# Mamba layer with routed experts: head and first batch rebuilt (one root for both norms, softplus by halves, C's rows through DRAM, states summed in three banks, other work dealt to other steps)

## The chip, the cores and the metric

One NeuronCore of a Trainium2 chip. The metric is the device time of one execution in microseconds. A core has TensorE (PE, matmuls into eight PSUM banks of 128 x 512 fp32), VectorE (DVE), ScalarE (ACT), GpSimd (POOL) and SyncE (SP, which here only issues transfers). Each engine runs its own instruction list in order; semaphores tie them together.

## The reference

x is 8 batches x 512 times x 128 features. Its layernorm xn goes into two branches, whose results are added to x:

```
a mamba block:
    xh = xn * rsqrt(mean(xn^2) + eps) * norm_w
    xs, z = split(xh @ in_proj.T)                  # 256 channels each
    u = silu(conv4(xs) + conv_b)                   # over time, per channel
    dt, B, C = split(u @ x_proj.T)                 # 8, 16, 16
    delta = softplus(dt @ dt_proj.T + dt_b)
    h[t,:,s] = exp(delta*A[:,s]) * h[t-1,:,s] + delta*u*B[t,s]     # 16 states
    y = sum_s C[t,s] * h[t,:,s] + u * D
    out = (y * silu(z)) @ out_proj.T + xn
eight experts, the two best for each of the 4096 rows (softmax of their two logits):
    out = sum_e gate[e] * (silu(xn @ w_gate[e]) * (xn @ w_up[e])) @ w_down[e]
```

## The kernel before, in words

**Mamba.** Channels lie on the partitions (two halves `hf` of 128), time along the 512 elements. Batches b = 0..7 come one after another, each in 16 steps k, one state each. Step n = 16b + k needs a decay exp(delta*A) (`decay`, `decay_bank` on ScalarE), an input delta*u*B and a scan by VectorE for each half. B's and C's values vary along time alone. They reach 128 partitions in two ways: as columns, when the input is turned (time on partitions), scaled by ScalarE (`scaled`) and turned back by TensorE (`dbu_turn`), or as rows read from DRAM with a broadcast (`rows_in`, `out_rows_in` on SP's queue), when GpSimd multiplies (`scaled` there). Batch 0 and most of batches 6 and 7 take the first way (`BY_PE`), the rest the second.

The sum over states has two forms. In batches 1 to 7 the scan writes in a PSUM bank, VectorE multiplies with C's row (`product`, L1055 to 1064) and TensorE adds the product, turned, in banks 2 and 3 (`accumulate`); `skip` adds u*D there. In batch 0 the scan writes in SBUF (`scan0`), TensorE turns h (`h_turn`), and VectorE multiplies by C's column and adds (`sums`, L1066 to 1078), four instructions a step. At its end `y_evac` (ScalarE) and `y_turn` (TensorE) bring y back to channels, with D's matmul, before `gate`.

**Head.** `stats` and `norms` (VectorE) give mean, 1/sigma and 1/rms for the first 4 tiles of 128 rows (batch 0) and then for the other 28, with two trips to ScalarE's square root each (`root`). VectorE writes xh, GpSimd xn (`normal`) and first the four scaled convolution weights wk. TensorE turns xh (`xh_turn`), ScalarE copies it (`xh_out`), four matmuls (`conv`) for each half make the convolution, then `silu`, `rows` (B, C, dt), `steps_mm` (delta's argument), and softplus as max(v,0) + ln(1 + exp(-|v|)) with a correction for what 1 + y rounds off: `magnitudes`, `vanishing`, `rounded`, `corrected`, `logarithm` on ScalarE, `remainder`, `softplus`, `input_scale` on VectorE for batch 0 and on GpSimd for the rest. `columns` makes the columns of B and C, `input_turn` turns delta*u.

**Routing**, in batch 0's steps: logits by TensorE; `choices` (VectorE, step 4) finds the two best of 8; GpSimd makes `sel`; TensorE `totals` and `ranking` (steps 5, 6), each copied by ScalarE (`routing`). GpSimd then works out each row's slot, the one-hot `hi_val` for half of the groups and each tile's expert (`texp`), L795 to 826. VectorE makes the other one-hots (`one_hots`, steps by `HOT_STEP`), TensorE multiplies them (`inverse`, `MAP_STEP`), `sources` gives the gather lists. Only after its chain does GpSimd work on batch 1: `remainder`, `softplus`, `input_scale`, `scaled(S)`, then it loads the first expert inputs. 72 expert tiles of 128 rows run beside the steps, one a step, from (b=1, k=2) to (5, 9) (`SLOTS`); SP loads their weights when `texp` is known. From (5, 14) on GpSimd gathers the results.

**Order.** Every engine's list is written out by step: `step0(k)` for batch 0 and `step(b, k)` for the others stand once per engine, and a table such as `HOT_STEP`, `SLOTS`, `COLS_AT` says in which step a piece is dealt with. `ST_LN`, `ST_RSTD` and so on count VectorE's small norm instructions for those who wait for one. SP's list: x in four parts (the second waits for ScalarE's five constant loads, `FIRST`), ten constants (`REST`), xn's rows to DRAM, rows of batch 1, weights. What sets a step's pace in the banked form:

```
wait(act, "p_rdy", freed(b, m))                       # L495: a decay waits for the product that read its bank
act.wait_ge(s["h_rdy"], 2 * IN_SBUF[i - ND] + hf + 1) # L452: one of three SBUF decays is free
wait(dve, "acc_mm", 2 * (S * (b - 1) + k - 1))        # L1060: a product waits for the sum two steps back
```

## Time and profile before

| | before |
|---|---|
| median of 3 runs | 686.74 us (684.6 to 687.96) |
| profiled execution | 688.27 us, span 686.4 us |
| busy share: PE, DVE, ACT, POOL | 80%, 89%, 63%, 77% |
| mean granted TensorE clock | 0.913 |
| chain that ended last, by engine | PE 41%, DVE 20%, ACT 15%, POOL 11%, issue 11%, DMA 3% |
| HBM read, written | 108.21 MB, 9.37 MB |

The time of an execution is its span, from the first to the last instruction, and a little around it. A row of a timeline gives the start in us from the span's start, the length from the first to the last of the instructions that it merges, engine, line, operation, tiles, shapes and count; in brackets the idle time before it and what ended it. A row of windows gives the stretch, its length, the busy time (and instructions) of PE, PE's weight loads, DVE, ACT and POOL, the granted clock, the DMA engines' busy share and GB/s. `bank` stands for any of the eight PSUM banks. A line of a helper serves several batches. The granted clock is 1.00 for TensorE's upper level, 2.4 GHz, and 0.50 for its lower, 1.2 GHz. A single matmul of fp32 shows as two instructions.

### The profile page before, as it was taken

Reading aid. Unit: us, or ns where it says so; the run is one execution under the profiler, and the core shown is the slowest. Engines: PE = TensorE matmul, PEld = TensorE weight load, DVE = VectorE, ACT = ScalarE, POOL = GpSimd, SP = SyncE. Lnnn points to the kernel's source line nnn. Section 1 sums busy time; section 2 is a strip of 40 time slices with the busy share of each in tenths; the row PEclk is TensorE's granted clock in tenths of the full one; section 3 lists DMA queues with packets and bytes.
Section 4 is the critical chain, followed back from the end, with each engine's and each line's share of the span. In section 5 each row is a group of like instructions: output and inputs, shape, how many; then the busy total and the mean of one; then the engine's idle time right before and its main releaser. Section 6 shows DMA issues by size and latency. Waiting matters only on the chain.

```text
span 686.4 us, 11312 instructions
## 1 busy us (share of the span) xinstructions
PE 547.6 (80%) x3456; PEld 425.1 (62%) x3456; DVE 613.3 (89%) x901; ACT 433.2 (63%) x849; POOL 528.8 (77%) x535
## 2 busy tenths in 40 slices
PE   2778767648879998899979998899887675687787
PEld 1256555435767877678767777687665454574554
DVE  6674888997998999999999999999999988888776
ACT  2498787614765576565765586657664689578680
POOL 5596059987988879896989879897869879758670
PEclk9958887767989999999999999999999897889987
DMA  6120040050776687687877687777843343223621
GB/s 203 54 62 16 1 187 1 0 192 16 255 249 236 230 288 252 211 251 275 290 251 267 236 302 265 227 278 232 295 145 147 147 157 141 81 78 108 161 77 31
DMA packets 58283, 118.32 MB, mean 172 GB/s; under 512 B 8200, under 2 KB 39440, under 8 KB 51440
## 3 DMA queue, kind: packets, MB, share of 16 engines
q1 hardware_dynamic: 53008, 107.83, 45.1%
q0 software_dynamic: 4496, 9.45, 5.4%
q8 instruction: 28, 0.46, 0.3%
q10 hardware_dynamic: 720, 0.33, 0.2%
q14 instruction: 31, 0.25, 0.1%
HBM read 108.21 MB, written 9.37 MB: 171 GB/s over the span
## 4 chain that ended last, share of the span: by engine, by line
PE 41%; DVE 20%; ACT 15%; POOL 11%; issue 11%; DMA 3%; DVEq 0%; ACTq 0%; POOLq 0%
DVE bank L1052 7%; PE bank L1330 7%; PE bank L1424 7%; PE bank L1306 5%; POOL dbu L845 5%; PE bank L1438 4%; PE bank L1432 4%; POOL xhT L874 3%; DVE h_sb L1063 3%; ACT dbu L487 3%; PE bank L1262 2%; ACT da L456 2%; PE bank L1353 2%; DVE h_sb L1034 2%; DMA xhT<-y_slots,slot 2%
## 5 line engine op out<-in xcount | busy, mean ns | idle before, releaser
L845 POOL TENSOR_TENSOR dbu<-du,xn_all 128x512 f32<-128x512 f32 x178 | 223.5, 1278 | 46.4 <-DVE bank L1052 45.9
L1052 DVE TENSOR_TENSOR_SCAN bank<-bank,dbu 128x512 f32<-128x512 f32 x176 | 214.2, 1221 | 4.1 <-ACT bank L471 4.1
L471 ACT ACTIVATE bank<-delta,a_sb 128x512 f32<-128x512 f32 x176 | 121.6, 692 | 99.1 <-DVE h_sb L1063 77.6
L1063 DVE TENSOR_TENSOR h_sb<-bank,xh_all 128x512 f32<-128x512 f32 x224 | 148.8, 676 | 1.1
L1306 PE MATMUL bank<-id_sb,h_sb 128*128 128x128 f32 x864 | 118.6, 283 | 16.8 <-DVE h_sb L1063 13.7
L1306 PEld LDWEIGHTS bank<-id_sb,h_sb 128*128 128x128 f32 x864 | 102.2, 147 | 25.9 <-DVE h_sb L1063 19.2
L1424 PEld LDWEIGHTS bank<-wd_sb,hid 117*128 117x128 f32 (+1 forms) x432 | 56.1, 194 | 64.1 <-issue 33.0
L1424 PE MATMUL bank<-wd_sb,hid 117*128 117x128 f32 (+1 forms) x432 | 66.0, 290 | 32.3 <-ACT xT L628 18.3
L1262 PE MATMUL bank<-id_sb,dbu 128*128 128x128 f32 x304 | 52.6, 315 | 38.0 <-ACT dbu L487 21.0
L832 POOL DMA_INDIRECT xs<-xn_rows,src x72 | 70.8, 983 | 14.2 <-issue 7.3
L1262 PEld LDWEIGHTS bank<-id_sb,dbu 128*128 128x128 f32 x304 | 40.4, 162 | 60.6 <-ACT dbu L487 31.9
L1330 PE MATMUL bank<-xhT,wk_sb 128*128 128x512 f32 x128 | 69.3, 673 | 1.7 <-ACT xhT L430 0.8
L1052 DVE TENSOR_TENSOR_SCAN bank<-da,bank 128x512 f32<-128x512 f32 x46 | 54.6, 1217 | 16.7 <-PE bank L1262 11.3
L487 ACT ACTIVATE dbu<-du_t,bc_sb 128x256 f32<-128x256 f32 x152 | 64.3, 496 | 1.3 <-PE bank L1262 1.2
L1432 PE MATMUL bank<-xT,wgu_sb 128*118 128x128 f32 x432 | 60.6, 277 | 4.2 <-DVE ga L1105 4.2
L456 ACT ACTIVATE da<-delta,a_sb 128x512 f32<-128x512 f32 x80 | 53.8, 713 | 13.5 <-DVE h_sb L1034 7.0
L1438 PE MATMUL bank<-xT,wgu_sb 128*118 128x128 f32 x432 | 60.5, 276 | 0.0
L1432 PEld LDWEIGHTS bank<-xT,wgu_sb 128*118 128x118 f32 x432 | 52.9, 184 | 6.6 <-issue 6.5
L874 POOL DMA_INDIRECT xhT<-y_slots,slot x48 | 46.7, 974 | 12.4 <-issue 11.7
L1438 PEld LDWEIGHTS bank<-xT,wgu_sb 128*118 128x118 f32 x432 | 53.9, 185 | 0.8 <-issue 0.8
L634 ACT ACTIVATE th<-bank 118x384 f32<-118x384 f32 x72 | 34.8, 484 | 29.3 <-PE bank L1432 26.9
L1034 DVE TENSOR_TENSOR_SCAN h_sb<-da,bank 128x512 f32<-128x512 f32 x30 | 34.9, 1202 | 18.4 <-issue 7.6
(191 smaller groups left out, 938.0 us busy)
## 6 DMA issues: line engine op xcount, KB each, us to landing
xh_all<-b_rows SPq DMA_DIRECT2D x28, 1024.0 KB
xn_all<-b_rows SPq DMA_DIRECT2D x25, 1024.0 KB
wgu_sb<-in_w_gu SPq DMA_DIRECT2D x72, 352.0 KB
wd_sb<-in_w_dn SPq DMA_DIRECT2D x72, 192.0 KB
y_slots<-ys SPq DMA_DIRECT2D x72, 64.0 KB
xn_rows<-xn_all SPq DMA_DIRECT2D x8, 256.0 KB, 2.3
out<-x_sb SPq DMA_DIRECT2D x7, 256.0 KB
x_sb<-in_x SPq DMA_DIRECT2D x2, 640.0 KB, 5.8
```

Of the source, the lines that this page charges most:

```text
L471: nc.scalar.activation(bank_of(b, m)[:, :], delta[b % 2][:, hf, :], ACT.Exp, scale=a_sb[:, hf, k:k + 1]).then_inc(s["da_rdy"], 1)
L487: last = nc.scalar.activation(dbuT[k % 2][:, t, :], duT[:, t, :], ACT.Copy, scale=bc_sb[q][:, t, k:k + 1])
L832: nc.gpsimd.indirect_dma_start(xs[i][:, :], None, xn_rows, bass.IndirectOffsetOnAxis(ap=src[:, j:j + 1], axis=0)).then_inc(s[f"xs_in{i}"], 16)
L845: nc.gpsimd.tensor_tensor(dbu[k % 2][:, hf, :], du[b % 2][:, hf, :], b_ring[c % 2][:, k % CH, :], ALU.mult).then_inc(s["dbu_p"], 1)
L1052: nc.vector.tensor_tensor_scan(at, da_of(n)[:, hf, :] if n in IN_SBUF else at, inp, 0.0, ALU.mult, ALU.add).then_inc(s["h_rdy"], 1)
L1063: nc.vector.tensor_tensor(h_sb[k % 2][:, hf, :], bank_of(b, 2 * k + hf)[:, :], c_ring[c % 2][:, k % CH, :], ALU.mult).then_inc(s["p_rdy"], 1)
L1262: last = nc.tensor.transpose(at[:, t * P:(t + 1) * P], dbuT[k % 2][:, t, hf * P:(hf + 1) * P], id_sb[:, :])
L1306: last = MM(HT[i][:, t % 2, hf * P:(hf + 1) * P], h_sb[k % 2][:, hf, t * P:(t + 1) * P], id_sb[:, :], is_transpose=True, start=(k == 0 and ...
L1330: last = MM(at[:, :], wk_sb[:, tap, hf * P:(hf + 1) * P], xhT[:, c, tap:tap + T], start=(tap == 0), stop=(tap == K - 1))
L1424: last = MM(XD[:, P:P + H], hid[j % 2][0:FN[c], c * P:(c + 1) * P], wd_sb[j % NW][0:FN[c], c, :], start=(c == 0), stop=(c == NF - 1))
L1432: last = MM(GB[0:FW, c * P:(c + 1) * P], wgu_sb[j % NW][:, c * FS:c * FS + FW], xT[j % 2][:, :], start=True, stop=True)
L1438: last = MM(UB[0:FW, c * P:(c + 1) * P], wgu_sb[j % NW][:, F + c * FS:F + c * FS + FW], xT[j % 2][:, :], start=True, stop=True)
```

## The change

It rewrites the head and batch 0; the 16 steps of the other batches keep their form.

- Norms: both variances (var + eps, and var*(1+eps') + eps*eps', under the root of which stands the product of both norms) go through one root, as a [128, 2, n] tensor. xh's scale is one of the two results. The 28 later tiles' rows are written in three parts (up to tile 24 in the head, 24 to 27 in step 0, 28 to 31 in step 1). 1/rms is worked out in step 1.
- The constants are loaded in another order; TensorE's and GpSimd's first wait is for three (`FIRST`), not five. The first convolution takes its taps from the last to the first, as GpSimd finishes them.
- Softplus of batch 0: by halves. ScalarE does Abs, Exp and Ln; VectorE max(v,0) from the bank, 1+y, the correction. Convolutions of batch 1 stand before the input is turned; its SiLU becomes tanh and a VectorE `unit`.
- Batch 0's state sum takes the form of the other batches, with three banks (0, 1, 5) as batches 6 and 7 have. C's rows for steps 0 to 7 come from DRAM in four pieces of two rows (512 KB spread over 128 partitions each) in buffers that are free then (`own`); those for steps 8 to 15 in `c_ring`. D is added by `skip` in steps 10 and 11.
- `choices` moves from step 4 to 7, totals and ranking from 5, 6 to 8, 9, one-hots from 9 to 14 to 12 to 15, the last two inverses and `sources` in step (1,0). Batch 1's softplus on GpSimd goes ahead of the routing chain, the first expert loads after step (1,0).
- Expert tiles start at (1,4) and end at (5,11). The columns of batch 6 are made two steps later.

The diff, cut to what this text speaks of:

```diff
-    TURNED, SKIPPED = 11, (1, 2)
+    TURNED, SKIPPED, SKIPPED0 = 11, (1, 2), (10, 11)
     LN_EPS = 1e-5
     RMS_EPS = float(np.finfo(np.float32).eps)
-    ST_LN, ST_RMS, ST_RSTD, ST_NORM = 7, 15, 12, 22
+    ST_ROOT, ST_NORM = 6, 13
+    XH_HEAD = 24
...
-        SLOTS = [(1, k) for k in range(2, S)] + [(b, k) for b in (2, 3, 4) for k in range(S)] + [(5, k) for k in range(10)]
+        SLOTS = [(1, k) for k in range(4, S)] + [(b, k) for b in (2, 3, 4) for k in range(S)] + [(5, k) for k in range(12)]
...
-        HOT_STEP = {9: (0, 1), 10: (2,), 11: (3,), 12: (4, 5), 13: (6,), 14: (7,)}
-        MAP_STEP = {10: (0, 1), 11: (2,), 12: (3,), 13: (4, 5), 14: (6,), 15: (7,)}
+        HOT_STEP = {12: (0, 1), 13: (2, 3), 14: (4, 5), 15: (6, 7)}
+        MAP_STEP = {13: (0, 1), 14: (2, 3), 15: (4, 5)}
+        def b_turn(k):
+            return {0: 4, 2: 5, 3: 6, 5: 7}.get(k)
...
-        COLS_AT = {5: 13, 6: 14}
+        COLS_AT = {5: 15, 6: 14}
...
-            return {9: 1, 12: 0} if b == 0 else {8: 1, 10: 0} if b == 6 else {4: 1, 6: 0}
+            return {13: 1, 15: 0} if b == 0 else {8: 1, 10: 0} if b == 6 else {4: 1, 6: 0}
...
-            return DAB2[m % 2] if b < 6 else DAB3[m % 3]
+            return DAB2[m % 2] if 0 < b < 6 else DAB3[m % 3]
...
+        own = [delta[1][:, 0:2, :], du[1][:, 0:2, :], g_sb[:, 0:2, :], u_sb[2][:, 0:2, :]]
...
-        FIRST, REST = 16 * 5, 16 * 10
+        FIRST, REST = 16 * 3, 16 * 10
...
+            def own_rows(i):
+                if i == 0:
+                    sp.wait_ge(s["b_st"], 16)
+                    sp.wait_ge(s["w_scaled"], 5)
+                spread_rows(own[i].rearrange("p s t -> p (s t)"), S + 2 * i, 2).then_inc(s[f"c_own{i}"], 16)
...
+            rows_kept(0)
+            rows_out(0)
+            for i in range(4):
+                own_rows(i)
+            for b in range(1, 4):
+                rows_kept(b)
+            sp.wait_ge(s["xh_pe"], 4)
+            out_rows_in(0, 2)
+            for b in range(4, NB):
+                rows_kept(b)
             rows_out(1)
+            sp.wait_ge(s["xh_pe"], NB)
+            out_rows_in(0, 3)
...
+            for dst, src_of in ((win_sb[:, :], w_in), (nw_sb[:, :], norm_w), (id_sb[:, :], ident)):
                 act.dma_start(dst, src_of).then_inc(s["in_first"], 16)
+            for dst, src_of in ((cb_sb[:, :], conv_b), (dtb_sb[:, :], dt_b)):
...
+                if 0 < k < S - 1:
+                    scaled(k + 1)
                 if k + 2 < S:
                     decay(k + 2)
                 elif k + 1 == S:
                     decay_bank(S, 0)
-                if 0 < k < S - 1:
-                    scaled(k + 1)
+                if b_turn(k) is not None:
+                    xh_out(b_turn(k))
+                if k in (0, 2):
+                    half_tanh(1, k // 2)
+                if k == 4:
+                    rows(1)
+                if k in (5, 6):
+                    magnitudes(1, k - 5)
+                    vanishing(1, k - 5)
+                if k == 6:
+                    rounded(1)
+                    corrected(1)
+                if k == 7:
+                    logarithm(1)
+                if k in (8, 11):
+                    half_tanh(2, k // 11)
...
+            def first_logarithm(hf):
+                act.wait_ge(s["sp_one"], hf + 1)
+                nc.scalar.activation(sp_e[:, hf, :], sp_d[:, hf, :], ACT.Ln).then_inc(s["sp_ln"], 1)
...
             silu(0, 0)
...
+            root(ST_NORM + ST_ROOT, slice(TT, NT))
             silu(0, 1)
...
             xh_out(1)
...
             act.wait_ge(s["in_rest"], REST)
             nc.scalar.activation(a_sb[:, :, :], a_sb[:, :, :], ACT.Exp).then_inc(s["a_ready"], 1)
...
+            rows(0)
+            xh_out(2)
+            for hf in range(NH):
+                magnitudes(0, hf)
+                vanishing(0, hf)
+            nc.scalar.activation(cbh_sb[:, :], cb_sb[:, :], ACT.Copy, scale=0.5)
             act.wait_ge(s["a_ready"], 1)
             nc.scalar.activation(a_sb[:, :, :], a_sb[:, :, :], ACT.Copy, scale=-1.0).then_inc(s["a_ready"], 1)
...
+            act.wait_ge(s["w_scaled"], 6)
+            first_logarithm(0)
+            first_logarithm(1)
             columns(0)
...
             act.wait_ge(s["a_ready"], 2)
             decay(0)
+            xh_out(3)
             input_turned(0)
             scaled(1)
             decay(1)
...
             for k in range(S):
...
+            remainder(pool, nc.gpsimd, 1)
             pool.wait_ge(s["oh_out"], 1)
             nc.gpsimd.tensor_tensor(sel[:, :, :], oh1, oh2, ALU.add).then_inc(s["sel_rdy"], 1)
             rt(nc.gpsimd.tensor_tensor(kk[:, :], m2[:, :], m1[:, :], ALU.subtract))
             nc.gpsimd.tensor_tensor(kk[:, :], kk[:, :], irms[:, :], ALU.mult).then_inc(s["top_rdy"], 1)
+            softplus(pool, nc.gpsimd, 1, 1)
+            input_scale(pool, nc.gpsimd, 1, 1)
             pool.wait_ge(s["rk_out"], 1)
...
+            def first_loads():
+                pool.wait_ge(s["xn_out"], 16 * NB)
+                pool.wait_ge(s["src_rdy"], 1)
+                for j in range(NXS - 1):
+                    load(j)
...
+                    if b == 1 and k == 0:
+                        first_loads()
...
+                var, a = [v[:, sl] for v in tmp]
+                under, root, inv, b = [v[:, :, sl] for v in both]
                 begun = cnt[0]
                 dve.wait_ge(s["stats_bn"], n1)
...
                 st(nc.vector.tensor_tensor(a, me, mo, ALU.subtract))
...
+                st(nc.vector.tensor_tensor(var, stat[:, sl, 2], stat[:, sl, 5], ALU.add))
                 st(nc.vector.scalar_tensor_tensor(a, a, 0.25, a, ALU.mult, ALU.mult))
...
+                st(nc.vector.scalar_tensor_tensor(var, var, 1.0 / H, a, ALU.mult, ALU.add))
+                st(nc.vector.tensor_scalar(both[0][:, 0, sl], var, LN_EPS, None, ALU.add))
+                st(nc.vector.tensor_scalar(both[0][:, 1, sl], var, 1.0 + RMS_EPS, LN_EPS * RMS_EPS, ALU.mult, ALU.add))
+                assert cnt[0] == begun + ST_ROOT
+                st(nc.vector.tensor_tensor(mean[:, sl], me, mo, ALU.add))
+                st(nc.vector.tensor_scalar(mean[:, sl], mean[:, sl], 0.5, None, ALU.mult))
+                dve.wait_ge(s["rms_rt"], roots)
+                st(nc.vector.reciprocal(inv, root))
+                st(nc.vector.tensor_tensor(b, inv, inv, ALU.mult))
+                st(nc.vector.tensor_tensor(b, b, under, ALU.mult))
+                st(nc.vector.tensor_scalar(b, b, -0.5, 1.5, ALU.mult, ALU.add))
+                st(nc.vector.tensor_tensor(inv, inv, b, ALU.mult))
...
+                if b == 0 and c < 2:
+                    if k % 2 == 0 and hf == 0:
+                        dve.wait_ge(s[f"c_own{k // 2}"], 16)
+                    row = own[k // 2][:, k % 2, :]
+                else:
+                    if k % CH == 0 and hf == 0:
+                        dve.wait_ge(s[f"c_in{c % 2}"], 16 * ((b - 1) * 2 + c // 2 + 2) if b else 16)
+                    row = c_ring[c % 2][:, k % CH, :]
                 if hf == 0:
...
+                    wait(dve, "acc_mm", 2 * (S * b + k - 1))
                 dve.wait_ge(s["h_rdy"], 2 * (b * S + k) + hf + 1)
...
+                nc.vector.tensor_tensor(h_sb[k % 2][:, hf, :], bank_of(b, 2 * k + hf)[:, :], row, ALU.mult).then_inc(s["p_rdy"], 1)
...
             def step0(k):
-                scan0(k)
-                if k > 0:
-                    sums(k - 1)
+                scan(0, k, 0)
+                scan(0, k, 1)
+                product(0, k, 0)
+                product(0, k, 1)
+                if k == 0:
+                    rows_normed(XH_HEAD, NT - TT)
+                if k == 1:
+                    rows_normed(NT - TT, NT)
+                    st(nc.vector.reciprocal(irms[:, :], sxh))
+                    st(nc.vector.tensor_tensor(irms[:, :], irms[:, :], rstd, ALU.mult))
+                if k in (0, 2):
+                    unit(1, k // 2)
+                if k == 7:
+                    choices()
+                if k in (8, 11):
+                    unit(2, k // 11)
+                if k == 10:
+                    weights()
                 if k in z_step(0):
                     z_gate(0, k)
-                if k == 4:
-                    choices()
-                if k == 10:
-                    weights()
                 for r in HOT_STEP.get(k, ()):
                     one_hots(ORDER[r])
-                if k in (11, 14):
-                    unit(2, k // 14)
-                if k == S - 1:
-                    sources()
...
+                if b == 1 and k == 0:
+                    sources()
...
+            relu(0)
+            one_more(0)
+            lost(0)
+            relu(1)
+            one_more(1)
+            regained(0)
+            lost(1)
+            first_step(0)
+            input_scale(dve, nc.vector, 0, 0, (0,))
+            regained(1)
+            first_step(1)
+            input_scale(dve, nc.vector, 0, 0, (1,))
             dve.wait_ge(s["row_mm"], 1)
-            for hf in range(NH):
-                dve.wait_ge(s["du_rdy"], hf + 1)
-                nc.vector.tensor_tensor(dbu[0][:, hf, :], du[0][:, hf, :], DBU[0][:, :], ALU.mult).then_inc(s["dbu_0"], 1)
+            first_input(0)
+            first_input(1)
...
             def step0(k):
                 if k > 0:
...
+                    dbu_turn(0, k, (1,))
+                    accumulate(k - 1)
+                if k + 1 < S:
+                    dbu_turn(0, k + 1, (0,))
                 for r in MAP_STEP.get(k, ()):
                     inverse(r)
                 if k == 1:
...
+                    conv(1, 1, range(K))
+                if k == 3:
                     rows(1)
...
+                if k == 7:
+                    conv(2, 0, range(K))
+                if k == 8:
+                    totals()
+                if k == 9:
+                    ranking()
+                if k in (9, 10):
+                    conv(2, 1, (2 * k - 18, 2 * k - 17))
                 if k + 1 in z_step(0):
                     z_mm(0, k)
...
+                if k in SKIPPED0:
+                    skip(0, (SKIPPED0.index(k),))
+                if b_turn(k) is not None:
+                    xh_turn(b_turn(k))
+                    logits(b_turn(k) - 1)
+                if k == 6:
+                    logits(NB - 1)
+                if k in (4, 5):
+                    steps_mm(1, k - 4)
...
             def step(b, k):
                 g = b * S + k
                 prev, here, nxt, nn = tile(g - 1), tile(g), tile(g + 1), tile(g + 2)
                 if k == 0:
-                    if b > 1:
-                        accumulate(g - 1)
+                    accumulate(g - 1)
+                    if b == 1:
+                        inverse(6)
+                        inverse(7)
...
-            pe.wait_ge(s["w_scaled"], 5)
-            pe.wait_ge(s["x_pad"], 2)
             pe.wait_ge(s["xhT_c"], 1)
             for hf in range(NH):
-                conv(0, hf, range(K))
+                conv(0, hf, range(K - 1, -1, -1))
+            xh_turn(1)
             rows(0)
-            xh_turn(1)
+            xh_turn(2)
             for hf in range(NH):
                 steps_mm(0, hf)
+            MM(bank[0][:, :], id_sb[0:2 * S, 0:1].to_broadcast([2 * S, P]), bct_full[0:2 * S, :],
+               start=True, stop=True).then_inc(s["row_mm"], 1)
             logits(0)
-            MM(DBU[0][:, :], id_sb[0:2 * S, 0:1].to_broadcast([2 * S, P]), bct_full[0:2 * S, :],
-               start=True, stop=True).then_inc(s["row_mm"], 1)
+            logits(1)
             columns(0)
-            logits(1)
-            xh_turn(2)
+            conv(1, 0, range(K))
+            xh_turn(3)
             input_turn(0, 0)
             logits(2)
-            xh_turn(3)
             for k in range(S):
                 step0(k)
             for b in range(1, NB):
```

## Rows read from the trace of the kernel before

**Rows 1.** Windows, all engines: head, batch 0; the third: batch 7's sixteen steps.

```profile
0.00:48.06 48.06, 26.90 (x63) 13.33 (x64) 32.18 (x118) 23.53 (x33) 31.74 (x49) 0.82 0.38 110
48.06:156.51 108.45, 77.81 (x443) 56.91 (x441) 89.04 (x135) 69.46 (x126) 72.59 (x96) 0.81 0.18 65
...
611.43:679.30 67.87, 52.34 (x283) 36.77 (x282) 56.66 (x68) 46.80 (x105) 42.67 (x55) 0.90 0.33 93
```

**Rows 2.** Timeline of VectorE, head and first steps: start, us, operation [idle before].

```profile
6.40 0.17 DVE L950 TENSOR_SCALAR tmp<-tmp 128x4 f32<-128x4 f32 x1
...
12.05 1.27 DVE L963 TENSOR_SCALAR xh_all<-x_sb,mean,sxh 128x128 f32<-128x128 f32 x4
...
30.18 7.88 DVE L963 TENSOR_SCALAR xh_all<-x_sb,mean,sxh 128x128 f32<-128x128 f32 x28
...
44.35 1.29 DVE L406 TENSOR_TENSOR delta<-sp_d,sp_m 128x512 f32<-128x512 f32 x2 [1.07 <-ACT sp_d L692]
...
57.57 2.33 DVE L1034 TENSOR_TENSOR_SCAN h_sb<-da,bank 128x512 f32<-128x512 f32 x2 [7.16 <-PE bank L1262]
```

**Rows 3.** Timeline of TensorE in the head.

```profile
14.63 6.66 PE L1330 MATMUL bank<-xhT,wk_sb 128*128 128x512 f32 x8 [0.78 <-ACT xhT L430]
22.07 3.70 PE L1330 MATMUL bank<-xhT,wk_sb 128*128 128x512 f32 x8 [0.78 <-ACT u_sb L645]
...
31.98 3.77 PE L1353 MATMUL bank<-bct_full,dtw_sb 8*128 8x512 f32 x4
```

**Rows 4.** Groups of VectorE over batch 0: name, count, busy us, mean ns, idle before.

```profile
L1077 DVE SCALAR_TENSOR_TENSOR g_sb<-bank,bc_sb,g_sb 128x256 f32<-128x256 f32 x56 | 22.8, 468 | 0.0
L1002 DVE TENSOR_TENSOR lo_oh<-lanes_sb,lo 128x1024 f16<-128x1024 f32 x8 | 11.4, 1432 | 0.0
```

**Rows 5.** Timeline of GpSimd, from the head to the end of its routing chain.

```profile
7.82 0.48 POOL L748 TENSOR_SCALAR wk_sb<-sp_e,nw_sb 128x256 f32<-128x256 f32 x1 [4.99 <-DMA dtb_sb<-in_dt_b]
...
91.38 0.20 POOL L795 TENSOR_SCALAR tiles<-wgu_sb 128x8 f32<-128x8 f32 x1 [5.77 <-ACT wgu_sb L441]
...
101.47 12.15 POOL L820 TENSOR_SCALAR hi_val<-lanes_sb,hi 128x72 f16<-128x72 f32 x16 [0.23 <-POOL lo L813]
...
136.96 2.49 POOL L387 TENSOR_TENSOR sp_m<-sp_m,sp_y 128x512 f32<-128x512 f32 x2
139.41 3.49 POOL L393 TENSOR_TENSOR sp_m<-sp_m,sp_e 128x512 f32<-128x512 f32 x2
```

**Rows 6.** Transfers issued in the first 60 us: KB each, median us to landing.

```profile
xn_rows<-xn_all SPq DMA_DIRECT2D x8, 256.0 KB, 2.3
...
g_sb<-in_conv_w POOLq DMA_DIRECT2D x1, 512.0 KB, 5.9
```

**Rows 7.** Timeline of ScalarE: the head's table load, two groups of a step.

```profile
41.97 1.28 ACT L692 ACT_TABLE_LOAD   x1
...
66.14 1.69 ACT L487 ACTIVATE dbu<-du_t,bc_sb 128x256 f32<-128x256 f32 x4
...
68.21 1.32 ACT L456 ACTIVATE da<-delta,a_sb 128x512 f32<-128x512 f32 x2
```

**Rows 8.** Timeline of VectorE in batch 7: scans of two successive steps.

```profile
614.86 2.33 DVE L1052 TENSOR_TENSOR_SCAN bank<-da,bank 128x512 f32<-128x512 f32 x2
...
618.28 2.33 DVE L1052 TENSOR_TENSOR_SCAN bank<-da,bank 128x512 f32<-128x512 f32 x2
```

**Rows 9.** Timeline of VectorE in batch 0: an instruction of `choices`.

```profile
79.28 0.42 DVE L974 TENSOR_REDUCE m<-wgu_sb 128x32 f32<-128x256 f32 x1
```

**Rows 10.** Windows of TensorE: busy, granted clock (share of full), DMA share, GB/s.

```profile
86.00:88.00 2.00, 2.00 (x11) 0.50 0.13 33
```

**Rows 11.** Groups of GpSimd up to the end of batch 0: busy, mean ns, waits.

```profile
L820 POOL TENSOR_SCALAR hi_val<-lanes_sb,hi 128x72 f16<-128x72 f32 x32 | 23.3, 750 | 2.1 <-PE bank L1245 1.8 <-POOL lo L813 0.2
```

**Rows 12.** Timeline of VectorE, first steps of batch 1.

```profile
156.51 1.22 DVE L1052 TENSOR_TENSOR_SCAN bank<-bank,dbu 128x512 f32<-128x512 f32 x1
...
163.69 1.28 DVE L1086 TENSOR_TENSOR g_sb<-zs_sb,bank 128x512 f32<-128x512 f32 x2 [3.29 <-PE bank L1390]
...
168.62 1.22 DVE L1052 TENSOR_TENSOR_SCAN bank<-bank,dbu 128x512 f32<-128x512 f32 x1
```

324 lines of the change are left out of this document (114 added, 210 removed).

## The prediction

> **What bounds the kernel now.** I read first how long each batch takes. The first scan starts at 48.06 us, batch 0 ends at 156.51, and in these 108.45 us VectorE is busy for 89.04 only [rows 1]. What follows, 530 us for seven batches, is nearly untouched by the diff. So the two prologue stretches are the question: 48.06 and 108.45 us, of 686.4.
>
> In the head the reader is to see a single chain that goes round VectorE, ScalarE, TensorE and GpSimd: the first normalised rows are written at 12.05, the other 28 only at 30.18, and delta only at 44.35; then scan 1 waits 7.16 us for its transposed input [rows 2]. TensorE runs its first convolution half from 14.63 in 6.66 us, the second from 22.07 in 3.70, the step matmuls of both halves from 31.98 in 3.77 [rows 3]. The first 6.66 and the 3.77 are slow for their size: the engine was at the lower level there.
>
> In batch 0 each step costs VectorE two scans and four sums; 56 of the 64 sum instructions keep it busy for 22.8 us, so all 64 for 26.1 [rows 4]. Last I read GpSimd's routing chain: it starts at 91.38, when the ranks are out of the bank, and gives way to the next batch's softplus at 136.96, 45.6 us later [rows 5].
>
> **The head.** (1) One root for both norms: 6 instructions before the root in place of 7, 7 after it (2 of them hidden beside it) in place of 16, and no second trip to ScalarE. The last instruction before the first root starts at 6.40; one of 0.2 us less before it, root and hand-overs of 0.4, then five of 0.2: the first rows can start at about 8.0, against 12.05 [rows 2]. Three transfers in place of five gate the scaled weights, whose first instruction starts at 7.82 on GpSimd [rows 5]; but the taps, 512 KB, take 5.9 us to land [rows 6] from their issue at the start, so I take only 0.5 us there. Some VectorE instructions next to GpSimd's get longer, so rows at 8.3 and the convolution at 10.9, against 14.63: 3.7 us won. The taps in falling order hide what is left of the scaling. (2) The convolution halves stay 6.66 and 3.70 [rows 3]: they end at about 22. (3) The second root waits behind the first SiLU, so the other rows come at about 21 in place of 30.18 [rows 2]; the turned inputs of the next batches, which stood in front of the step matmuls, no longer wait for them. B and C's rows are in SBUF at about 26. (4) Softplus by halves: step matmul about 1 us at the upper level (1.9 in the trace, 3.77 for two [rows 3]), then ScalarE Abs and Exp for each half, 4 x 0.65 (two 128x512 instructions take 1.32), one table load of 1.28 and two Ln halves of 0.6 [rows 7]: the logarithms are done at about 32.5. Relu, 1+y and the correction run on VectorE meanwhile. After the first Ln half come seven VectorE instructions at 0.64 (1.29 for two [rows 2]), 4.5 us: scan 0 at about **37**, 11 us earlier. If TensorE works at the lower level again, as it did for the 3.77, two step matmuls and the columns behind them cost 2 to 3 us more.
>
> C's rows need a store and a load by DRAM. The store waits for the 26 above. The nearest rows are a store of 256 KB, 2.3 us to landing, and the load of the taps to all partitions, 512 KB as each of these four, 5.9 us [rows 6]. That puts the first pair in SBUF at 35, and the first product is due at 39.5. Cost 0; if the four loads queue behind each other, 4 x 5.9 us is still before step 6. At most 3 us, which I keep for the range.
>
> **Batch 0.** (5) VectorE: 89.04 busy, less 26.1 of sums, plus 32 products. A step of two scans and two products in this very form is in batch 7: 614.86 to 618.28 is 3.42 us [rows 8], so the products add 16 x 1.2 = 19. Moved in: 8 normalised rows at 0.28 (7.88 for 28 [rows 2]), two u multiplications and the reciprocal, 4 us. The one-hots ran 1.43 us at a mean where 1.22 is their quick length [rows 4], since GpSimd's softplus ran beside them; that softplus is earlier now: 4 us less with their companions. Sum 82: VectorE alone would need 82 us where 108.45 stood.
>
> (6) It won't be alone. ScalarE has for every step four scaled copies (1.69) and two decays (1.32), 2.9 us when they follow each other closely [rows 7]; to these come in steps 0 to 7 fifteen 128x512 instructions of about 0.65 (inputs turned, half-tanhs, the magnitudes of batch 1), two of 1.15 and a Ln with its table: 14.4 us. So 38 us in eight steps, against VectorE's 8 x 3.42 + 4 = 31. I work each step through its queue: product k-1 frees the bank, TensorE sums it and turns the next input, ScalarE delivers one step ahead. Scan 1 starts 8 us after scan 0 (in place of 9.5), step 7 ends at about 73. `choices` then costs 12 instructions at 0.42 with 0.03 between them [rows 9], 5.4: about 78.
>
> (7) From there the routing sets the end. GpSimd makes `sel`, TensorE totals, ScalarE copies, TensorE ranks, ScalarE copies. Before, the second instruction of `choices` began at 79.28, so it ended near 84.3, and 91.38 is 7 us later [rows 5, 9]; now ScalarE has a half-tanh, scaled copies and decays in between, and TensorE has stood idle during `choices`, after which its granted clock was 0.50, the lower level [rows 10]. I take 10.5: ranks out at **88.5**. Of the 45.6 us of GpSimd's chain 2.1 were waits, 1.8 of them for slots [rows 11]; the rest stays: about 43.5. Softplus of batch 1 is past by then, so `scaled(S)` follows at once and its first half takes 1.3. Batch 1's first scan: 88.5 + 43.5 + 1.5 = **133.5**, against 156.51. VectorE has finished batch 0 at about 127 and waits 6 us. So 23 us won, 11 in the head, 12 in batch 0.
>
> The GpSimd row to weigh here: its `hi_val` instructions take 12.15/16 = 0.76 us each in their first sixteen, and the correction, with one-hots beside it, takes 1.75 each where the sum before it takes 1.25 [rows 5]. The Trainium skill (GPSIMD Engine Reference, Specifications) says that GpSimd shares its SBUF interfaces with VectorE and contends with instructions that have two SBUF inputs; the trace agrees, and the change now packs all one-hots into steps 12 to 15.
>
> **After batch 0.** (8) The end of the state sum no longer waits for four `sums`, a y turned and a D matmul: the gate's wait of 3.29 before 163.69 goes [rows 12]. But `sources` now follows the gate, and GpSimd makes four gathers after it and then the input of step 2: about 12 us to step 2, as before (156.51 to 168.62 [rows 12]). 0. (9) Two expert tiles move from steps (1,2), (1,3) to (5,10), (5,11). A step with a tile is longer than one without by the same amount at either place, as VectorE paces both: net 0. But the gather of slots keeps its step, two steps after the last tile in place of four, and the columns of batch 6 come two steps later, behind which TensorE turns batch 6's input. 1 to 2 us, taken as 1.5. SP's added transfers (a store, six row loads) stand before waits that are met anyway. The row loads are bounded by nothing and 3 us.
>
> **Sum**, against the profiled execution's 688.27 (span 686.4): -23 + 1.5 = -21.5, so 666.8. That execution lies 1.5 above the median 686.74; against the median it gives **665**.
>
> **Rivals.** *VectorE sets the end of batch 0* (0.18): the routing hand-overs take the old 7 us and the queue is level, step 7 ends at 70: VectorE's 82 us plus 5 of stalls, a start at 126 to 128. 659. For it: VectorE was the busiest engine of batch 0 [rows 1].
> *Port sharing stretches GpSimd's chain* (0.13): 16 us of two-input one-hots beside `hi_val` and the 8 expert comparisons, each longer by 1.75/1.25: 16 x 0.4 = 6 us more on the very chain that sets the end. 671. The rule of the Trainium skill (GPSIMD Engine Reference, Key points) would give this; against it, most of the 45.6 us already include such overlap.
> *The loop of three banks paces the steps* (partial 0.12; fully 0.04). Scan k needs a bank freed by a product, filled by TensorE, from ScalarE's copy. Batch 7, the same form, takes 67.87 us with 56.66 busy [rows 1]: 11.2 us idle in 16 steps. The same on top of my queues gives +8, 673. If every step lost 1.6 us beyond my working, 16 x 1.6 = 25 us, the whole gain is gone; at 2 us, 697 at a start of 166: **slower**. It decides from 1.6 us a step. Batch 7 shows 0.7.
> *The gain doesn't arrive* (0.03): expert weights or gathers are late in batch 1 and VectorE stands there; about 685.
>
> **Numbers.** Main case 0.50, 660 to 671. Together with the faster rival and the partial one, and the bounds above (3 for rows, 3 for the clock, 3.5 for hand-overs), 655 to 676 holds 8 in 10. Over 0.5%, 3.4 us, is what a measurement here can tell: faster 0.93, same 0.04, slower 0.03.
>
> **What would show it.** First rows near 8.3, scan 0 near 37, the first product without a wait for C's rows; step 7 ends near 73; ranks out near 88.5; VectorE's long wait at batch 1's first scan ended by GpSimd's `dbu`; batches 2 to 4 as long as before. Wrong if VectorE's wait there is absent (rival one), if the `hi_val` instructions average above 0.9 us (rival two), or if VectorE idles in every step for TensorE or ScalarE (rival three).

## The result and the profile after

| | before | after |
|---|---|---|
| median of 20 executions each | 686.95 us (682.66 to 692.81) | 682.92 us (672.99 to 690.37) |
| profiled execution, span | 688.27, 686.4 us | 673.05, 671.2 us |
| mean granted TensorE clock | 0.913 | 0.919 |

The forecast was 665 (655 to 676). The changed kernel's twenty times fall into two groups with nothing between them: ten from 672.99 to 680.1 and ten from 685.74 to 690.37. The medians of all stand at 682.92/686.95 = 0.994. The ratio with an interval, 0.9857 [0.9833, 0.988], leaves the upper ten out, as every ratio here does with executions over 1.5% above the fastest. The profiled execution is of the lower group, and is one of its three shortest (the median of the ten is 676.7); it shows the steps of the forecast undisturbed. The upper group is the main finding.

Windows of after, all engines (head, batch 0, batch 7), to be read against [rows 1]:

```profile
0.00:37.95 37.95, 24.67 (x77) 12.30 (x78) 29.08 (x97) 19.23 (x29) 24.05 (x39) 0.96 0.60 173
37.95:141.03 103.08, 77.50 (x457) 59.05 (x455) 86.34 (x113) 65.22 (x126) 78.79 (x105) 0.82 0.18 65
594.00:665.60 71.60, 53.05 (x287) 37.99 (x288) 59.23 (x72) 49.19 (x109) 42.49 (x55) 0.93 0.32 89
```

The head won 10.1 us (48.06 to 37.95), its clock in these rows rose from 0.82 to 0.96 (they show 1.00 up to 17.3 us, yet the first five instructions of the convolution stand 0.85 us apart and the later ones 0.43, so TensorE still began at its lower level); batch 0 won only 5.4 (108.45 to 103.08). VectorE is 84% busy there, against 82% before.

Timeline of after, the rows that answer to [rows 2, 3, 5, 12]:

```profile
10.26 1.17 DVE L993 TENSOR_SCALAR xh_all<-x_sb,mean,both 128x128 f32<-128x128 f32 x4
12.72 5.95 PE L1387 MATMUL bank<-xhT,wk_sb 128*128 128x512 f32 x8 [0.69 <-ACT xhT L461]
19.45 3.70 PE L1387 MATMUL bank<-xhT,wk_sb 128*128 128x512 f32 x8 [0.78 <-ACT u_sb L674]
22.58 5.58 DVE L993 TENSOR_SCALAR xh_all<-x_sb,mean,both 128x128 f32<-128x128 f32 x20
37.95 2.37 DVE L1072 TENSOR_TENSOR_SCAN bank<-da,dbu 128x512 f32<-128x512 f32 x2
40.23 1.26 DVE L1089 TENSOR_TENSOR h_sb<-bank,delta 128x512 f32<-128x512 f32 x2
...
78.60 0.41 DVE L1002 COPY wgu_sb<-bank 128x256 f32<-128x256 f32 x1
...
102.79 27.18 POOL L856 TENSOR_SCALAR hi_val<-lanes_sb,hi 128x72 f16<-128x72 f32 x32 [0.23 <-POOL lo L849]
...
141.03 1.23 DVE L1072 TENSOR_TENSOR_SCAN bank<-bank,dbu 128x512 f32<-128x512 f32 x1 [7.56 <-POOL dbu L881]
...
153.39 1.23 DVE L1072 TENSOR_TENSOR_SCAN bank<-bank,dbu 128x512 f32<-128x512 f32 x1 [3.30 <-POOL dbu L881]
```

Scan 0 stands at 37.95, the first product follows without a wait for C's rows, `choices` begins at 78.60, and VectorE's long wait ends with GpSimd's `dbu`: the forecast's picture, 7.5 us late.

### The profile page after: what moved, and what is told of

Same layout as the page of the kernel before. It is cut to its first block, busy times and chain, and to the rows that moved or that the text cites. A ratio compares the mean times of both kernels' runs of the same rounds, so it can differ in the third digit from the quotient of the medians.

```text
span 671.2 us, 11273 instructions
## 1 busy us (share of the span) xinstructions
PE 540.2 (80%) x3468; PEld 425.2 (63%) x3468; DVE 607.5 (91%) x859; ACT 424.4 (63%) x841; POOL 528.3 (79%) x535
## 4 chain that ended last, share of the span: by engine, by line
PE 42%; ACT 19%; DVE 15%; POOL 13%; issue 11%; DMA 1%; DVEq 0%; ACTq 0%; POOLq 0%
DVE bank L1072 7%; PE bank L1481 7%; PE bank L1387 7%; PE bank L1355 6%; ACT dbu L514 5%; PE bank L1495 4%; POOL dbu L881 4%; PE bank L1489 4%; POOL hi_val L856 4%; ACT da L486 4%; DVE h_sb L1089 3%; PE bank L1318 2%; PE bank L1410 2%; PE bank L1456 2%; PE bank L1367 1%
## 5 line engine op out<-in xcount | busy, mean ns | idle before, releaser
L1355 PE MATMUL bank<-id_sb,h_sb 128*128 128x128 f32 x992 | 144.2, 293 | 24.2 <-DVE h_sb L1089 13.1
L1089 DVE TENSOR_TENSOR h_sb<-bank,xh_all 128x512 f32<-128x512 f32 x240 | 160.3, 682 | 1.2
L1355 PEld LDWEIGHTS bank<-id_sb,h_sb 128*128 128x128 f32 x992 | 123.0, 152 | 36.8 <-DVE h_sb L1089 20.9
L1072 DVE TENSOR_TENSOR_SCAN bank<-da,bank 128x512 f32<-128x512 f32 x76 | 90.2, 1217 | 23.0 <-PE bank L1318 21.5
L1318 PE MATMUL bank<-id_sb,dbu 128*128 128x128 f32 x304 | 55.0, 313 | 38.3 <-DVE h_sb L1089 20.5
L1387 PE MATMUL bank<-xhT,wk_sb 128*128 128x512 f32 x128 | 64.3, 634 | 1.5 <-ACT u_sb L674 0.8
L486 ACT ACTIVATE da<-delta,a_sb 128x512 f32<-128x512 f32 x80 | 54.1, 712 | 8.6 <-DVE bank L1072 6.0
L910 POOL DMA_INDIRECT xhT<-y_slots,slot x48 | 46.6, 971 | 14.9 <-issue 11.5
L667 ACT ACTIVATE ys<-bank 128x128 f32<-128x128 f32 x72 | 19.8, 274 | 39.9 <-PE bank L1481 28.9
```

The lines of the kernel that those rows point to most:

```text
L486: nc.scalar.activation(da_of(n)[:, hf, :], delta[b % 2][:, hf, :], ACT.Exp, scale=a_sb[:, hf, k:k + 1]).then_inc(s["da_rdy"], 1)
L1072: nc.vector.tensor_tensor_scan(at, da_of(n)[:, hf, :] if n in IN_SBUF else at, inp, 0.0, ALU.mult, ALU.add).then_inc(s["h_rdy"], 1)
L1089: nc.vector.tensor_tensor(h_sb[k % 2][:, hf, :], bank_of(b, 2 * k + hf)[:, :], row, ALU.mult).then_inc(s["p_rdy"], 1)
L1318: last = nc.tensor.transpose(at[:, t * P:(t + 1) * P], dbuT[k % 2][:, t, hf * P:(hf + 1) * P], id_sb[:, :])
L1355: last = MM(HT[i][:, t % 2, hf * P:(hf + 1) * P], h_sb[k % 2][:, hf, t * P:(t + 1) * P], id_sb[:, :], is_transpose=True, start=(k == 0 and ...
L1387: last = MM(at[:, :], wk_sb[:, tap, hf * P:(hf + 1) * P], xhT[:, c, tap:tap + T], start=(tap == taps[0] if c == 0 else tap == 0), stop=(ta ...
```

## The experiments

Each line of medians is compared with before on the same chip. On some chips before takes 687 to 688, on others 679: theories are told apart within a chip. "Before takes" names the median of the kernel before on that chip.

### The changed kernel again, and GpSimd's input put first

The first has no edit. The second takes the inputs of steps (1,0) and (1,1) out from behind the expert comparisons:

```diff
+            scaled(S)
+            scaled(S + 1)
             for e in range(E):
                 rt(nc.gpsimd.tensor_scalar(tkey[:, :, e], ...
...
-            scaled(S)
```

> The changed kernel once more, unchanged, to see how its times spread and whether batch 1 always starts where the first trace shows it (141.0 us). Theory A (GpSimd's routing chain sets the start of batch 1, and little else differs): 673 to 680 us in each run, batch 1's first scan at 141 with VectorE's wait of 7.6 us before it ended by GpSimd's dbu. Theory B (something apart from the chain takes about 14 us in many runs, as the times from 673 to 690 suggest): two clusters, near 675 and near 688, and if a trace of the upper cluster is seen, a stall of 10 us or more that the first trace does not have.

> Batch 1's first two inputs are multiplied by GpSimd ahead of the eight expert comparisons (9.7 us), and the first four gathers are dealt to steps (1,1) to (1,3). Theory A (the chain sets the start): the first scan of batch 1 comes at 133.5 to 135 in place of 141, the wait before it shrinks from 7.6 to about 1 us, and the time falls by 3 to 6 us against the unchanged one (some is given back at the third step, which waits for the comparisons and its own input). Rival (VectorE or TensorE have no slack there, or the later batches set the time): the same time within 1 us. Theory B says nothing on the first scan, but keeps two clusters 14 us apart.

Measured, where before takes 679.0: 680.48 (671.67 to 683.61), 0.9992 [0.9947, 1.0037]; and 672.27 (three executions at 667.5 to 667.7, three at 676.8 to 680.8), 0.9891 [0.9836, 0.9946]. The six times of the unchanged kernel (671.67, 677.63 and four from 680.08 on) decide nothing between A and B; its trace is of the shortest, with the first scan of batch 1 at 140.68. The second kernel has two groups again, 9 to 13 us apart, and this time the profile caught the upper one, so it can't show what theory A expected of the first scan. Its time is not in waits: up to batch 1's gate VectorE idles less than in the trace of after (22.6 us against 25.8), but is 11.7 us longer busy (130.8 against 119.1), 8.4 of it in one instruction. The timelines of VectorE and GpSimd at this place, first the kernel with the input first (upper group), then after (lower group), then GpSimd in before:

```profile
49.78 9.52 DVE L996 TENSOR_SCALAR xh_all<-x_sb,mean,both 128x128 f32<-128x128 f32 x4
49.81 8.64 POOL L803 TENSOR_TENSOR x_sb<-x_sb,xn_all 128x512 f32<-128x512 f32 x7
59.22 0.34 DVE L1146 RECIPROCAL irms<-both 128x32 f32<-128x32 f32 x1
59.38 1.26 POOL L803 TENSOR_TENSOR x_sb<-x_sb,xn_all 128x512 f32<-128x512 f32 x1 [0.93 <-DVE xh_all L996]
```

```profile
49.10 2.66 DVE L993 TENSOR_SCALAR xh_all<-x_sb,mean,both 128x128 f32<-128x128 f32 x4
50.41 9.90 POOL L803 TENSOR_TENSOR x_sb<-x_sb,xn_all 128x512 f32<-128x512 f32 x8
52.06 0.91 DVE L1144 TENSOR_TENSOR irms<-irms,both 128x32 f32<-128x32 f32 x1
```

```profile
52.68 9.90 POOL L770 TENSOR_TENSOR x_sb<-x_sb,xn_all 128x512 f32<-128x512 f32 x8
```

And the rows of the line alone, with the shortest, median and longest of its 32 instructions, in the same order:

```profile
L996 DVE TENSOR_SCALAR xh_all<-x_sb,mean,both x32: 332/390/8750, 10.4 to 59.0; 128x128 f32<-128x128 f32 x32
```

```profile
L993 DVE TENSOR_SCALAR xh_all<-x_sb,mean,both x32: 332/390/1335, 10.3 to 50.4; 128x128 f32<-128x128 f32 x32
```

One instruction that takes 0.39 us took 8.75, the first of the last four rows. It began beside the first of GpSimd's eight sums x + xn, seven of which follow each other without a gap, and it ended when the seventh did; the eighth needs these four rows, so GpSimd paused, and both went on. In after it was the last of the four that met the first sum, and it lost that sum only, 1.33 us. The profile calls VectorE busy throughout. In before these rows were all written by 38.1 (30.18 + 7.88 [rows 2]) and GpSimd's sums began at 52.68: the two could not meet. The change moved the last rows into step 1.

### Taking the rows out of the meeting, and forcing them into it

Theory H (a hold) says that this one instruction makes the upper group.

```diff
+            pool.wait_ge(s["xh_w"], NT)
             for b in range(NB):
                 pool.wait_ge(s["xh_w"], b * TT + TT)
```

> Edit: GpSimd starts its eight sums of x and xn only when VectorE has written all normalised rows. It adds a wait of about 1 us to an engine that is idle from 60 to 73 us. Theory H (a hold): in the run of 676.84 VectorE's last rows began after GpSimd's first 128x512 sum and one of them took 8.75 us instead of 0.39, which is the whole upper group of times; the changed kernel's own upper group has the same cause. H expects every run in one group, at the changed kernel's lower times: 671 to 676, about 8 under the unchanged one's median of that chip and with a far smaller spread than 12 us; VectorE's rows at 49 us of 0.33 to 0.39 each. Rival N (noise of the chip or its clock, and the hold is rare): the same two groups, 672 and 680 to 684, and a ratio near 1.00 to before.

```diff
                 if k == 1:
+                    dve.wait_ge(s["acc_w"], 1)
                     rows_normed(NT - TT, NT)
```

> Edit: VectorE's last four normalised rows of step 1 wait until GpSimd has ended the first of its eight sums, so they always arrive in the middle of the chain. H: one of the four rows is held until the chain pauses before its eighth sum, 6 x 1.24 = 7.4 us, and the wait for the first sum adds 1 to 2.5; every run is in the upper group, 8 to 10 above the lower one: 681 to 685 in all runs, none under 679. N, or a hold of one instruction of GpSimd only: a row of 1.3 us, 674 to 677 in the lower runs.

The same with, in GpSimd's loop:

```diff
             for b in range(NB):
+                if b > 1:
+                    pool.wait_ge(s["acc_w"], b)
```

> Edit: as the one before, and each of GpSimd's sums after the second waits for the end of the one before it, so that the queue is not back to back. H in its strong form (the row waits for the end of GpSimd's running instruction, and only instructions that follow without a gap keep it out): the row gets in at the first gap and takes 1.3 to 2.6 us; times as the kernel with the wait for all rows plus 2 to 4. H in its weak form (GpSimd's sums keep VectorE's row out whatever stands between them): a row of some 7 to 8 us, and times of the upper group.

> Edit: the kernel that puts GpSimd's input of steps (1,0) and (1,1) ahead of the expert comparisons, with the wait of GpSimd's sums for all rows. H expects all runs at that kernel's lower times, 667 to 669, ratio to before 0.983; N expects its two groups again, 667.6 and 677 to 681.

All on one chip, before 687.6:

| kernel | median, all executions | ratio |
|---|---|---|
| sums wait for all rows | 677.0 (675.5 to 678.8) | 0.9859 [0.9822, 0.9895] |
| rows forced into the sums | 686.58 (684.9 to 690.8) | 0.9987 [0.9958, 1.0017] |
| forced, sums with gaps | 683.93 (680.9 to 686.0) | 0.9950 [0.9922, 0.9978] |
| input first, sums wait | 672.99 (671.3 to 675.4) | 0.9793 [0.9756, 0.983] |

H holds in all four: one group each, of the kind that it says. The medians of the first, second and fourth lie 1 to 4 us above the ranges given for them. With the rows kept out of the sums, every execution is in the lower group; forced together, ten of ten are in the upper. The unchanged kernel's upper group was never profiled itself, but it stands where the forced one does, which makes a hold in it very likely, though none was seen there. Timelines of the two forced kernels:

```profile
51.00 8.64 POOL L803 TENSOR_TENSOR x_sb<-x_sb,xn_all 128x512 f32<-128x512 f32 x7
52.31 8.18 DVE L993 TENSOR_SCALAR xh_all<-x_sb,mean,both 128x128 f32<-128x128 f32 x4 [2.27 <-POOL x_sb L803]
```

```profile
50.62 10.56 POOL L805 TENSOR_TENSOR x_sb<-x_sb,xn_all 128x512 f32<-128x512 f32 x8
51.91 5.32 DVE L995 TENSOR_SCALAR xh_all<-x_sb,mean,both 128x128 f32<-128x128 f32 x4 [2.32 <-POOL x_sb L805]
```

Without gaps one row is held 7.41 us, six sums. With a gap of 0.08 us between the sums (1.34 us from one to the next in place of 1.23) each of the four rows gets in at the next gap, 1.29 to 1.43 us each. The strong form of H stands, though my price for it was low: the time came out 6.9 us above the kernel whose sums wait, where I expected 2 to 4, because all four rows are held in turn (5.32 for 1.1) and the wait for the first sum adds 2.3.

The added wait of GpSimd takes only the rows out of the meeting. The 128x32 product for 1/rms, which comes behind them and takes 0.19 us alone, still runs into the first sum. Timeline of the kernel whose sums wait:

```profile
50.99 9.88 POOL L804 TENSOR_TENSOR x_sb<-x_sb,xn_all 128x512 f32<-128x512 f32 x8 [0.42 <-DVE xh_all L994]
51.20 1.11 DVE L1145 TENSOR_TENSOR irms<-irms,both 128x32 f32<-128x32 f32 x1
```

It began 0.21 us into the first sum here and in the seven other traces of kernels with this wait in which the two meet, and lost that one sum (1.10 to 1.12 us) each time. So the wait gives the meeting a fixed place where it was cheap; it doesn't remove it.

### Only the rows moved; the one-hots doubled; the experts on VectorE

```diff
-                    rows_normed(XH_HEAD, NT - TT)
+                    rows_normed(XH_HEAD, NT)
                 if k == 1:
-                    rows_normed(NT - TT, NT)
                     st(nc.vector.reciprocal(irms[:, :], sxh))
```

> Edit: the changed kernel with nothing but its last four normalised rows moved from step 1 of batch 0 to step 0, beside the twenty others' last four, 8 us before GpSimd's sums begin; no wait added. H: one group of times, the same as with the added wait: ratio to before 0.985 to 0.987, spread under 5 us, no VectorE row above 0.8 us. If the upper group had another cause that the added wait only happened to cover, half of the runs stand 8 to 12 us higher again.

This expectation fell: 674.53 (670.3 to 681.4), eight executions at 670 to 677 and four at 680 to 681.4, 0.9914 [0.9881, 0.9947], where before takes 678.5. The profiled one is of the upper four:

```profile
50.31 9.86 POOL L803 TENSOR_TENSOR x_sb<-x_sb,xn_all 128x512 f32<-128x512 f32 x8
50.53 0.35 DVE L1142 RECIPROCAL irms<-both 128x32 f32<-128x32 f32 x1
50.91 9.31 DVE L1143 TENSOR_TENSOR irms<-irms,both 128x32 f32<-128x32 f32 x1
```

The rows were gone, but the product behind them, with two inputs in SBUF, met the sums in their place: 9.31 us for 0.19. So it is not one instruction: a one-input row and a two-input product were both held. The 1/rms product is also what the wait of the sums leaves in their way. The reciprocal in front of it, one input of 128x32 in SBUF, began 0.22 us into the same first sum and kept its 0.35 us. VectorE's scans and products h x C, each with one input in a PSUM bank, keep their 1.22 and 0.68 us beside the same sums.

The doubled one-hots, on top of the kernel whose sums wait (the added one goes into scratch):

```diff
+                st(nc.vector.tensor_tensor(sp_e[...], lane128..., spread(lo[...])..., ALU.is_equal))
                 nc.vector.tensor_tensor(lo_oh[:, sl, :], ..., ALU.is_equal).then_inc(s["lo_rdy"], 1)
```

> Edit: on top of the kernel whose sums wait for all rows, each of VectorE's eight lo_oh comparisons of 128x1024 is issued twice (the first into scratch). It adds 8 x 1.25 = 10 us to VectorE. Theory P (GpSimd's routing chain was 3.5 us longer than predicted because its hi_val instructions, 0.58 us apart where nothing meets them, wait for VectorE's one-hots): the hi_val group grows from 27.2 to 32 to 36 us and batch 1's first gate moves from 146.4 to 151 to 154. Rival V (VectorE itself sets the end, GpSimd's chain does not care): hi_val stays at 27, VectorE's end of batch 0 moves by 10 against a slack of 7.6, and the gate by 2 to 3, to 149.

678.9, ratio 0.9995 [0.9969, 1.0021]. Groups of GpSimd in its trace:

```profile
L857 POOL TENSOR_SCALAR hi_val<-lanes_sb,hi 128x72 f16<-128x72 f32 x32 | 32.3, 1032 | 0.2 <-POOL lo L850 0.2
L860 POOL TENSOR_SCALAR wgu_sb<-lanes_sb,ends 1x72 f32<-1x72 f32 x8 | 8.7, 1093 | 0.7
```

against 27.2 and 6.7 in after, and 23.3 before [rows 11]. Theory P stands: 10 us more of VectorE's one-hots made GpSimd's chain from the ranks to `dbu` 54.1 us long (97.09 to 151.15) where after has 46.95 and the kernel whose sums wait 46.45 (94.69 to 141.14). The gate stands at 156.38, later than either theory said, since this chain also began 4.4 us later than in after.

Putting the input first, on top of the wait, won 4.0 us on one chip (677.0 to 672.99), but not where theory A had it: the first scan of batch 1 stands at 142.70 in its trace, against 142.54, and the input of step (1,2) comes 3.2 us earlier (151.65 for 154.89). The next two edits look at that first scan. The expert choice (eight comparisons, a tree, a minimum) on VectorE, on top of both edits, and then GpSimd's `dbu` behind VectorE's last one-hot:

```diff
+                st(nc.vector.tensor_tensor(tkey, lanes..., ends[1][0:1, E:2 * E]..., ALU.is_ge))
+                st(nc.vector.tensor_reduce(tsum[:, :], tkey, AX.X, ALU.add))
+                nc.vector.tensor_scalar(texp[:, 0:NJ], tsum[:, :], float(E - 1), None, ALU.min)...
```

```diff
+            pool.wait_ge(s["hi_rdy"], 4)
             scaled(S)
             scaled(S + 1)
```

> Edit: on top of the kernel with both edits (sums wait for all rows; GpSimd's input of steps (1,0) and (1,1) ahead of the expert comparisons), the eight comparisons, the three-level sum and the minimum that give each tile its expert leave GpSimd (10.1 us there) for VectorE: one comparison of 1x576, one reduction, one minimum, 1.6 us, in step 12 of batch 0. GpSimd goes from hi_val straight to dbu and then to the gathers. Theory H (a two-input VectorE instruction that arrives while GpSimd's 128x512 products follow each other waits for all of them): one of VectorE's last one-hots again takes about 6 us, as the 6.40 one of the kernel with both edits; the first scan of batch 1 then stands near 142 and only the later waits for dbu go: 1 to 3 us won against that kernel's 673.0 on the chip of that run (ratio to before 0.976). Rival: the 6.40 us one-hot was a chance meeting; first scan near 137, ratio 0.970.

> Edit: the kernel with the expert choice on VectorE, and GpSimd waits with dbu until VectorE's last one-hot of batch 0 is written. H: VectorE's one-hots take 1.22 each again, they end near 135, dbu's first half is there 1.3 us later and the first scan of batch 1 stands at 136 to 137: 5 us before the kernel without this wait, ratio to before 0.969 to 0.971. Rival (no hold between these two): the wait only delays dbu, and the kernel is 1 us slower than the one without it.

666.28 (662.8 to 670.0), 0.9795 [0.9754, 0.9835], and 664.63 (662.6 to 665.9), 0.9775 [0.9743, 0.9807], with before at 678.5. Both gains are smaller than expected (0.976 and 0.969 to 0.971). The hold shows again at this second place. Timeline of VectorE, without and with the wait:

```profile
134.18 5.79 DVE L1030 TENSOR_TENSOR lo_oh<-lanes_sb,lo 128x1024 f16<-128x1024 f32 x2
141.34 1.23 DVE L1077 TENSOR_TENSOR_SCAN bank<-bank,dbu 128x512 f32<-128x512 f32 x1
```

```profile
131.24 2.35 DVE L1031 TENSOR_TENSOR lo_oh<-lanes_sb,lo 128x1024 f16<-128x1024 f32 x2
136.59 1.23 DVE L1078 TENSOR_TENSOR_SCAN bank<-bank,dbu 128x512 f32<-128x512 f32 x1 [1.54 <-POOL dbu L877]
```

One of the two one-hots took 4.65 us, and 6.40 in the kernel with both edits; behind the wait both are quick and the scan stands at 136.6, as forecast. The gap between the medians, 1.65 us, is less than the 4.75 between these scans, of which 1.4 lay in the head, and the two intervals overlap: the traces show the hold gone, the times don't show what that is worth.

### Which queue paces steps 0 to 7

```diff
-                if k in (0, 2):
-                    half_tanh(1, k // 2)
+                if k in (1, 2):
+                    half_tanh(1, k // 2)
```

and `unit` on VectorE likewise; then also the z gate of (0,15) behind the one-hots.

> Edit: on top of the kernel with the expert choice on VectorE and the wait for its last one-hot, ScalarE's half-tanh and VectorE's u of (batch 1, half 0) move from step 0 to step 1 of batch 0. In the trace of that kernel VectorE stands 3.70 us before this u (45.32) while the bank of scan 1 is turned at 41.74. Theory Q (the pace of the first steps is set by what is queued in front of scan 1, not by TensorE or VectorE): scan 1 starts at 42.0 to 43.5 in place of 45.99, the end of choices moves by 1 to 3 us and so does the end: 662 to 664 on a chip where that kernel takes 664.6. Rival S (ScalarE's queue paces steps 0 to 7, which holds the same instructions in either order): scan 1 earlier, choices within 0.7 us of 79 to 84 as before, no change of the time beyond 1 us.

> Edit: on top of the one before, the z gate of step (0,15) goes behind VectorE's last one-hots. There it waited 0.68 for ScalarE's tanh, and it needs neither the shared path nor GpSimd's dbu, so it fills VectorE's wait of 1.54 for dbu. First scan of batch 1 1.3 to 1.5 us earlier after the end of choices; ratio against the one before 0.998.

666.48, 0.9812 [0.9781, 0.9842], and 667.77, 0.9838 [0.9815, 0.9862]. VectorE in the first of them:

```profile
41.96 1.23 DVE L1078 TENSOR_TENSOR_SCAN bank<-da,bank 128x512 f32<-128x512 f32 x1 [0.24 <-PE bank L1326]
...
49.14 5.40 PE L1395 MATMUL bank<-xhT,wk_sb 128*128 128x512 f32 x8 [2.51 <-DVE u_sb L1109]
55.08 1.23 DVE L1078 TENSOR_TENSOR_SCAN bank<-da,bank 128x512 f32<-128x512 f32 x1 [4.86 <-PE bank L1326]
```

Scan 1 came 4 us earlier than in the kernel they build on (45.99), as Q said, and `choices` began 3.5 us later (81.12 for 77.61): TensorE's convolution now waited for u in front of step 2's bank. Neither time came down: 662 to 664 was expected of the first, 0.998 of that for the second. So the three that follow, with these on one chip (before 679.2):

> Edit: none against the kernel with the expert choice on VectorE and GpSimd's wait for its last one-hot (0.9775 of before, 662.6 to 665.9). Expected again: 0.975 to 0.980 and a spread under 4 us; on a chip where before takes 687, 0.970 to 0.975.

> Edit: on top of it, only the z gate of step (0,15) behind VectorE's last one-hots. VectorE's 0.68 for the tanh and 0.69 of work move into its 1.54 wait for dbu: first scan of batch 1 at 135.1 in place of 136.6, the end 0.5 to 1.5 us earlier. If it shows nothing, the 1.4 us are taken back by batch 1's first states, which wait for GpSimd or the bank.

> Edit: on top of that, the half-tanh and u of (1, half 0) in step 1 as before, but TensorE's convolution (1, half 1), eight matmuls of 5.4 to 6.3 us behind which the turned bank of step 2 stood for 4.86 and 5.75 us of VectorE's time, moves to the end of its step 2, and u of (1, half 1) to step 3. Theory Q2 (an instruction queued in front costs its whole length, wherever it is put, and the cheapest place is behind the banks of the next step): scan 1 near 42, no wait of VectorE above 2 us until step 3, choices begins at 74.5 to 76.5 in place of 77.6, the end 1 to 3 us earlier. Rival S2 (ScalarE's queue, 38 us of work in steps 0 to 7, is the bound): choices begins at 77 to 78 whatever the order.

The edit of the last, beside `half_tanh` as above:

```diff
-                if k in (0, 2):
+                if k in (1, 3):
                     unit(1, k // 2)
...
-                if k == 1:
+                if k == 2:
                     conv(1, 1, range(K))
```

663.19 (661.3 to 668.0), 0.9787 [0.9749, 0.9825]; 664.77, 0.9795 [0.9765, 0.9825]; 665.83, 0.9809 [0.9776, 0.9843]. The first agrees with its first measurement in the ratio, not in the spread (6.7 us for under 4), and in its trace the first scan stands at 139.13, 2.5 us later than before. The gate edit brought batch 1's first scan to 135.39 as expected, and the segment up to the next gate grew by 1.2 us (74.96 to 76.15): taken back, as its alternative said. Windows of after and of the last kernel, from scan 0 to `choices`:

```profile
37.95:78.60 40.65, 34.08 (x195) 27.27 (x193) 34.24 (x45) 34.51 (x68) 26.01 (x27) 0.83 0.39 138
```

```profile
38.20:79.76 41.56, 34.72 (x197) 28.04 (x195) 32.24 (x45) 34.96 (x68) 26.40 (x28) 0.84 0.39 134
```

Q2's saving didn't come: scan 1 came forward (42.75), but a wait of 2.79 us opened in step 4, and `choices` begins at 79.76, where 74.5 to 76.5 was expected. How far an order moves this stretch can't be read from single traces. The order of after gave 40.6 us, the one with u later 44.0 and 44.7 (the gate edit lies outside the stretch), the last 41.6; but the order of after, in its ten traces in which no instruction of this stretch was held for more than one sum, gave 40.6 to 44.0 by itself (40.65 in after, 40.62 and 41.75 in the two traces of the kernel that these edits build on, 43.97 in the one with the input first and the sums waiting). Only the 44.7 lies outside. Nor is a bound shown: ScalarE idles over 6 us in each of the two rows above, and 40.6 came out at a granted clock of 0.83 in after and 0.92 in the kernel with the gate last. What sets it stays open.

### Before and after on one of the other chips

> Edit: none, the kernel before, for its trace on another chip. On two chips it took 679, on three others 687 to 688. If the 8 us lie in the last two batches (waits of VectorE for the last gathers) or are spread over the batches by the clock, this trace shows it beside the first one, when it is of the 679 group. If the time is 687 again, the trace gives its spread between chips of one group.

> Edit: the changed kernel with GpSimd's sums behind all normalised rows, again, on the chip of the other three runs. Theory H: every run within 4 us of the lowest, no VectorE row above 0.8 us in the trace. Against before it was 0.9859 on a chip where before takes 687.6; if this chip is of the 679 group it shows the gain there, expected 0.989 to 0.991 from the lower runs of the kernel with the early rows (670.3 to 673.1 against 678.5).

Before again: 679.9 (674.5 to 680.9); the changed kernel whose sums wait: 671.15 (670.9 to 676.2), 0.9906 [0.9879, 0.9933], five within 1.5 us and one 5 above the lowest, which is more than the 4 expected. The trace is of one of the five, with no row held and the 1/rms product at 1.10; the sixth wasn't traced. Before's span here is 674.9, 11.5 less than in its first trace, and two thirds of that lie in the last batch. Windows of batch 7, gate to gate, first before, then the kernel whose sums wait, both on this chip:

```profile
605.88:669.21 63.33, 48.98 (x287) 34.93 (x288) 58.64 (x71) 47.90 (x108) 42.55 (x55) 0.97 0.36 100
```

```profile
597.57:663.75 66.18, 51.73 (x287) 36.75 (x288) 58.53 (x72) 47.87 (x108) 42.52 (x55) 0.92 0.34 96
```

In the first traces the same stretch took 71.0 us (609.62 to 680.65) and 71.5. All traces of the changed kernel and its variants fall the same way: twelve traces on chips where before takes 679 have 66.1 to 66.8 us here, five where it takes 687 to 688 have 71.4 to 71.8. So on such a chip before gains 7.7 us in batch 7 (one trace of each kind) and the changed kernel 5.3; VectorE's idle time in it (length less busy) fell from 11.9 us (71.03 - 59.16) to 4.7 in before and from 12.3 (71.53 - 59.20) in after to 7.7 in the other. The clock of the stretch is 0.97 against 0.92. Why its waits for TensorE's banks are shorter there isn't settled, nor is the last 2.9 us between the two kernels; moving the expert tiles back by itself was not tried.

## Why the prediction was wrong

The forecast of the time failed twice: by 6.3 us that the traced execution of the lower group shows, and by the upper group.

**The step that failed is (5), "moved in: 8 normalised rows at 0.28".** It priced them at their quick length and asked only what VectorE pays, not what runs on GpSimd when they arrive. Four of them arrive at 49 to 50 us, where GpSimd's eight 1.23 us sums begin. The meeting costs 1 us or the rest of the sums, 7.4 to 8.8. The second is what separates the two groups of the kernel with the input first, 9 to 13 us apart, and what forced the upper group in ten of ten; that it also lifts half of the changed kernel's own executions by 12 us follows from these and wasn't traced. The port rival had the mechanism from the other side alone (GpSimd waits for one-hots, 6 us, 671), with each instruction longer by a share of itself, and counted two-input instructions, where a row is scaled from one tensor; no case held a VectorE instruction waiting for a whole queue.

**The 6.3 us**, from the lower group's trace, term by term:
- (1) to (4), the head: scan 0 at 37.95 for 37. Rows at 10.26 for 8.3, the small instructions beside GpSimd's being longer; given back in part by the convolution's 5.95 for 6.66 and the step matmuls at the upper level as forecast. C's rows cost nothing, as forecast. +0.95.
- (6), ScalarE's queue: scan 1 7.7 us after scan 0, as forecast, but steps 0 to 7 took 40.65 for 36. The waits for turned banks in steps 4 to 7 are 3.9 us of it. +4.65, the largest term. The working walked the queues once and took each as level after step 1; which queue sets the 40.65 the three orders tried did not show.
- (7), hand-overs: `choices` to the ranks' arrival 14.1 for 15.5. -1.4.
- (7), "the rest stays: about 43.5": 46.95. +3.45. `hi_val` took 27.2 us for 23.3: alone they stand 0.58 us apart, and eight of them, where five before, wait for a one-hot. The doubled one-hots confirm the cause. Before's 45.6, less 1.9 of waits and 0.6 of shorter expert comparisons, plus these 3.9, is the 46.95 within 0.1. This was the second rival's mechanism at half its size (0.87 us on average, under the 0.9 that I had set as its mark).
- (8) and (9): from batch 1's first scan to the end 530.17 us, before 529.89 (686.4 - 156.51): +0.3 for +1.5. -1.2.

The sum is 0.95 + 4.65 - 1.4 + 3.45 - 0.1 (the last `scaled`, 1.4 for 1.5) - 1.2 = 6.35, against the 6.25 between the profiled 673.05 and the forecast's 666.8 for such an execution. The trace of the kernel run again has the same four stretches within 0.5 us (38.07, 40.64, 14.12, 46.46), on another chip. But the lower group's median is 676.7, 3.6 above its profiled execution, while before's profiled execution lay 1.3 above its median, and the forecast took off 1.8 for that. So the terms above explain half of the 11.7 us between that median and 665; the rest is which execution was profiled, and what spreads the group from 673 to 680 stays open. The range to 676 held the profiled execution and three more of the ten, and not the median of all.

**The signs.** Faster holds for the lower group (0.9857); for all twenty, 0.994 on medians, it isn't shown, since half of them lie among before's own times. On a chip where before takes 679 the same kernel was no faster, 0.9992 [0.9947, 1.0037]. Two causes are likely there, a hold in some of the executions (not traced) and a last batch that gains less than before's. Rivals two and three each came in part, 3.45 us of 6 and 4.65 of 8; rival one did not happen, for VectorE waited 7.56 us. Rival three's mark was set too high: 665 is 21.7 below before's median, so 1.4 us a step, not 1.6, would have taken the whole gain. That this wait is near the 6 us forecast does not speak for the sizes: VectorE's queue ended 6.5 us late and the chain 7.5.

**A version better than both**: the changed kernel with the sums behind the rows, the input ahead, the expert choice on VectorE and `dbu` behind the last one-hot, 0.9775 [0.9743, 0.9807] and 0.9787 [0.9749, 0.9825] of before on two chips, against 0.9906 with the first edit alone on a third of the same kind.

## What to carry to other kernels

Price a moved VectorE instruction by what GpSimd runs at its new place, and look at the longest of a line, not its mean: 8.75 us in a group whose median is 0.39 shows as busy time, and no wait view has it. Where GpSimd issues large instructions without a wait between them, keep VectorE's row-scaling instructions on SBUF and two-input products out by an order, or leave gaps. A wait on the engine that is idle later was enough here (677.0, one group, in place of two), though it left one product in the sums' way; a wait behind that product as well was not tried. When one kernel's times come in two groups, profile until both are caught before explaining the median.

## What the runs showed of the hardware

A VectorE instruction on SBUF alone (a 128x128 row, a two-input product or comparison) that comes after GpSimd's first 128x512 sum waited for one sum (1.33, 1.11 and 0.91 us) or for all that followed without a gap (8.75, 9.31, 7.41, and 6.40 and 4.65 beside four products). With gaps of 0.08 us each of the four rows was let in at the next one. The Trainium skill (SBUF — State Buffer, Who interferes with whom) says that whoever comes first holds the pair of ports that VectorE and GpSimd share for the whole instruction and the other blocks; the traces agree for the single holds and differ in the others, where the block lasted for up to eight instructions. How far into a sum it arrived does not tell the two outcomes apart: 0.02, 0.21 (in eight traces) and 0.42 us in gave one sum, -0.03, 0.08 and 0.60 gave all. What does is open.

Nor is a missing gap enough. Beside GpSimd's `hi_val` instructions of 128x72, 0.58 us apart without a wait, VectorE's one-hots kept 1.21 to 1.28 us in after, and it was GpSimd that waited. And in the kernel with the input first, the last one-hots took turns with the very products of `dbu` that held them in the two later kernels:

```profile
141.48 7.50 POOL L876 TENSOR_TENSOR dbu<-du,xn_all 128x512 f32<-128x512 f32 x4
141.83 4.29 DVE L1035 TENSOR_TENSOR lo_oh<-lanes_sb,lo 128x1024 f16<-128x1024 f32 x2
```
